# A two-layer kernel (cross-attention, then an RWKV block): the group norm's two head products as rounded passes, and a new order within a step

## The reference, cut to what matters

```python
xa = _ln(x, ln1_w, ln1_b)                       # layer norm over channels
sx = concat([state[:, 1:2] - xa[:, :1], xa[:, :-1] - xa[:, 1:]])
xxx = einsum(tanh((xa + sx * maa_x) @ maa_w1), maa_w2)
xk, xw, xv, xr, xg = xa + sx * (maa_stack + xxx)
w = exp(-exp(time_decay + tanh(xw @ td_w1) @ td_w2))
r, k, v = xr @ Wr.T, xk @ Wk.T, xv @ Wv.T;  g = silu(xg @ Wg.T)
out_t = r_t (u * k_t v_t + s);  s = k_t v_t + w_t * s      # scan over the tokens
m = og.mean(-1);  va = ((og - m) ** 2).mean(-1)            # og: out by heads of 16
og = (og - m) / sqrt(va + 1e-5) * gn_w + gn_b              # the group norm
x1 = x + (og * g) @ Wo.T
xc = _ln(x1, ln2_w, ln2_b); xk2, xr2 = mixes of xc and its shift
out = x1 + sigmoid(xr2 @ Wfr.T) * (square(relu(xk2 @ Wfk.T)) @ Wfv.T)
```

## Time and profile before

| what | value |
|---|---|
| median of three executions | 1414.32 us (1409.76 to 1417.7) |
| the profiled execution's own time | 1411.06 us |
| its span in the trace | 1409.2 us |
| granted TensorE clock, mean over the span | 0.981 of full speed |
| busy: TensorE / weight loads | 1329.8 us (94%) / 936.5 us (66%) |
| busy: VectorE, ScalarE, GpSimd | 929.5 us (66%), 734.7 us (52%), 492.5 us (35%) |
| chain that ended last, by engine | PE 80%, DVE 8%, issue 6%, DMA 3% |

### The profile page before, as it was taken

How to read it: one execution, slowest core, us unless ns; L and a number is a source line. 1 busy time by engine, 2 the same in 40 slices (tenths; PEclk the granted TensorE clock), 3 DMA queues, 4 the chain that set the end, 5 groups by cost and what they waited for, 6 DMA issues and landing times.

```text
span 1409.2 us, 42786 instructions
## 1 busy us (share of the span) xinstructions
PE 1329.8 (94%) x17120; PEld 936.5 (66%) x17120; DVE 929.5 (66%) x2431; ACT 734.7 (52%) x1772; POOL 492.5 (35%) x550
## 2 busy tenths in 40 slices
PE   4899999999999999987899999999999999999977
PEld 4677777777777777655666667666676667666634
DVE  3455555555555555456578878787888787887863
ACT  4676766766777666542334443545344534543332
POOL 2322222222222211113455345634554355534540
PEclk9999999999999999989899999999999999999979
DMA  5433322222222222213000010001000101010000
GB/s 169 138 94 106 100 69 69 71 75 75 75 75 75 75 69 65 89 43 135 21 21 10 26 28 21 13 24 27 21 14 22 27 22 27 9 27 21 15 14 13
DMA packets 47145, 73.70 MB, mean 52 GB/s; under 512 B 21413, under 2 KB 24101, under 8 KB 45445
## 3 DMA queue, kind: packets, MB, share of 16 engines
q1 hardware_dynamic: 46981, 71.24, 16.8%
HBM read 60.24 MB, written 7.57 MB: 48 GB/s over the span
## 4 chain that ended last, share of the span: by engine, by line
PE 80%; DVE 8%; issue 6%; DMA 3%; SPq 1%; ACT 1%; POOL 1%; DVEq 0%; ACTq 0%; POOLq 0%
PE b_bank L1824 18%; PE b_bank L1830 12%; PE ring_bank L696 6%; PE ring_bank L697 5%; PE ring_bank L698 5%; PE av_bank L782 4%; PE b_bank L1938 4%; PE score_banks L755 4%; DVE probs L443 3%; PE b_bank L1975 3%; PE score_banks L742 2%; PE b_bank L1964 2%; PE b_bank L1878 2%; DVE probsT L460 2%; PE av_bank L768 2%
## 5 line engine op out<-in xcount | busy, mean ns | idle before, releaser
L1119 POOL TENSOR_TENSOR rst<-rp,st 128x448 f32<-128x448 f32 x192 | 210.1, 1117 | 59.6 <-DVE st L1342 57.7
L443 DVE CUSTOM_DVE_ANT_0 probs<-score_banks,unmask 112x375 f32<-112x375 f32 x256 | 124.8, 545 | 93.0 <-issue 93.0
L588 ACT ACTIVATE probs<-probs,least_inv 112x375 f32<-112x375 f32 x256 | 152.4, 606 | 32.6 <-DVE least_inv L443 32.6
L460 DVE SCALAR_TENSOR_TENSOR probsT<-score_banks,least_cols 125x448 f32<-125x448 f32 x192 | 108.0, 618 | 54.4 <-PE score_banks L755 51.7
L603 ACT ACTIVATE probsT<-probsT,key_mask 125x448 f32<-125x448 f32 x192 | 114.6, 661 | 47.9 <-DVE probsT L460 47.7
L1111 POOL TENSOR_TENSOR xm<-mixed,xa 128x448 f32<-128x448 f32 x80 | 88.5, 1107 | 143.6 <-DVE mixed L1271 137.3
L337 POOL TENSOR_TENSOR aT_lo<-whole,aT_hi 128x375 fp32r<-128x375 f32 x64 | 58.9, 920 | 194.7 <-ACT whole L569 192.6
L696 PE MATMUL ring_bank<-aT_hi,wk_lo 128*128 128x376 f32 x256 | 91.2, 356 | 2.4 <-issue 2.4
L371 POOL TENSOR_TENSOR ctx_rstd<-ctx_var_eps,a_eps_exp 125x3 f32<-125x3 f32 x16 | 13.8, 864 | 214.6 <-DVE ctx_var_eps L416 214.6
L697 PE MATMUL ring_bank<-aT_lo,wk_hi 128*128 128x376 f32 x256 | 85.5, 334 | 0.0
L698 PE MATMUL ring_bank<-aT_hi,wk_hi 128*128 128x376 f32 x256 | 85.4, 334 | 0.0
(11 more groups left out here) (183 smaller groups left out, 3108.5 us busy)
## 6 DMA issues: line engine op xcount, KB each, us to landing
least_cols<-values_of_two_batches SPq DMA_DIRECT2D x32, 437.5 KB
ctx_tok<-in_ctx SPq DMA_DIRECT2D x16, 750.0 KB
xT_sb<-in_xT SPq DMA_DIRECT2D x16, 224.0 KB, 3.0
inv_cols<-values_of_two_batches SPq DMA_DIRECT2D x128, 28.0 KB, 4.1
x_tok<-in_x SPq DMA_DIRECT2D x16, 224.0 KB, 2.6
x_between_layers<-x_tok SPq DMA_DIRECT2D x16, 224.0 KB, 4.5
b_x<-x_between_layers SPq DMA_DIRECT2D x16, 224.0 KB, 3.0
x_post<-x_between_layers SPq DMA_DIRECT2D x16, 224.0 KB, 2.8
```

Source lines behind the costliest of these rows:

```text
L443: dve.tensor_tensor_reduce(out=probs[:, g % 2, i], in0=score_bank[0:T, i, 0:TC], in1=unmask[:, m[1]], scale=-SCALE, scalar=-LOWEST, op0=AL ...
L460: dve.scalar_tensor_tensor(out=probsT[:, g % 2, k].rearrange("p (i t) -> p i t", t=T), in0=score_bank[0:TK, :, k * T:(k + 1) * T], scalar= ...
L588: act.activation(probs[:, g % 2, i], probs[:, g % 2, i], ACT.Exp, scale=-1.0, bias=least_at(m, g, i), accum_out=sums[:, g, i:i + 1]).then_ ...
L1119: pool.tensor_tensor(by_chunk(rst[:, j % NPROD]), by_chunk(rp[:].rearrange("p c t -> p (c t)")), state_of(j), ALU.mult).then_inc(s_pprod, 1)
```

## The change

Both products of the group norm are made of two passes in the rounded float format (fp32r) instead of one float32 product. `wkv` is split: ScalarE's new `norm_high` rounds it, GpSimd's new `norm_low` subtracts the rounded part, and TensorE's `gn_centre` multiplies both parts with a matrix `centring` (identity minus head mean), which gives the centred values at once; `gn_mean` and VectorE's `centre` are gone. The squares are split in the same way: `square` and the new `square_high` on ScalarE, `square_low` on GpSimd, then two passes in `gn_var`. `x2` shares its memory with `x1_post` and `fin` with `ln2_tok`; two constants share a semaphore.

From step 3 on the lists within a step are also in another order, on all five engines. Steps 1 and 2 keep the old order (`early_step`), with the new calls put in.

```diff
+        centring = sb_first("centring", [P, P], F32R)
+        mean_r = sb_first("mean_r", [P, P], F32R)
...
         def step(n, pre, scan, post):
             m = later(n, -1)
-            if post:
-                l = later(n, -2)
-                if at_least(l, 1):
-                    sp.wait_ge(s_x2, count(later(l, -1), 1, 1))
-                sp.dma_start(x1p[:], A["x1"][index(l)]).then_inc(s_x1p[l[1]], 16)
             if pre and not is_batch(n, B - 1):
                 load_x1(later(n, 1))
             if post and at_least(n, 3):
                 store_out(later(n, -3))
+            l = later(n, -2)
+            if post and not is_last(l):
+                if at_least(l, 1):
+                    sp.wait_ge(s_fin, count(later(l, -1), 1, 1))
+                sp.dma_start(x1p[:], A["x1"][index(l)]).then_inc(s_x1p[l[1]], 16)
             if pre:
                 spread_value(n)
...
+        def norm_low(l):
+            pool.wait_ge(s_gnhi, count(l, 2, 1))
...
+            low, high = norm_parts(l)
+            pool.tensor_tensor(low, wkv[:], high.bitcast(F32), ALU.subtract).then_inc(s_gnlo, 1)
+
+        def square_low(l):
+            pool.wait_ge(s_sq, count(l, 1, 1))
+            pool.wait_ge(s_gnhi, count(l, 2, 2))
+            pool.tensor_tensor(norm_parts(l)[1], norm_home(l)[1], wkv_r[:].bitcast(F32), ALU.subtract).then_inc(s_gnlo, 1)
...
-        def centre(l):
-            dve.wait_ge(s_mean, count(l, 1, 1))
...
-            dve.tensor_tensor(norm_home(l)[0].rearrange("p c t -> p (c t)"), wkv[:].rearrange("p c t -> p (c t)"),
-                              norm_bank(l)[0][:, 0:CT], ALU.subtract).then_inc(s_cen, 1)
...
             if scans:
+                prefixes(m)
                 for d in range(2, CH + 1):
                     decay_key(m, d)
                 near_products(m, 0)
-                near_products(m, 1)
-                prefixes(m)
-                near_products(m, 2)
             if more:
                 stats1(p)
             if post:
                 wkv_sum(l)
             if scans:
+                near_products(m, 1)
                 decay_rec(m)
             if post and at_least(n, 3):
                 finish(later(n, -3))
...
+        def norm_high(l):
+            act.wait_ge(s_wkv, count(l, 1, 1))
...
+            act.copy(norm_parts(l)[1], wkv[:]).then_inc(s_gnhi, 1)
...
+        def square_high(l):
+            act.wait_ge(s_cen, count(l, 1, 1))
+            act.activation(wkv_r[:].rearrange("p c t -> p (c t)"), norm_bank(l)[0][:, 0:CT], ACT.Square).then_inc(s_gnhi, 1)
...
-                copy_vtok(n)
             if post:
                 xc_affine(l)
             if more:
                 xa_affine(p)
             if pre:
-                copy_rec(n)
                 tanh_gate(n)
+                copy_vtok(n)
             if post:
                 relu_square(l)
                 receptance(l)
...
-        def gn_mean(l):
-            pe.wait_ge(s_wkv, count(l, 1, 1))
+        def gn_centre(l):
...
+            pe.wait_ge(s_gnlo, count(l, 2, 1))
...
-            pe.matmul(norm_bank(l)[0][:, 0:CT], headmean[:], wkv[:].rearrange("p c t -> p (c t)"), start=True,
-                      stop=True).then_inc(s_mean, 1)
+            low, high = (x.rearrange("p c t -> p (c t)") for x in norm_parts(l))
+            pe.matmul(norm_bank(l)[0][:, 0:CT], centring[:], high, start=True, stop=False)
+            pe.matmul(norm_bank(l)[0][:, 0:CT], centring[:], low, start=False, stop=True).then_inc(s_cen, 1)
...
-            pe.matmul(norm_bank(l)[1][:, 0:CT], headmean[:], norm_home(l)[1].rearrange("p c t -> p (c t)"), start=True,
-                      stop=True).then_inc(s_var, 1)
+            pe.matmul(norm_bank(l)[1][:, 0:CT], mean_r[:], high, start=True, stop=False)
+            pe.matmul(norm_bank(l)[1][:, 0:CT], mean_r[:], low, start=False, stop=True).then_inc(s_var, 1)
```

More of the change, by code:

```diff
@@ L1149, in last_steps @@
             rec_key(m)
+            norm_low(l)
+            square_low(l)
             product(m, 0)
@@ L1180, in step @@
                 mix(n, 1)
-            if early:
                 rstd1(p)
+            if post:
+                norm_low(l)
+                square_low(l)
             if scan:
@@ L1211, in step @@
                 xa_state(p)
+        def step(n, pre, scan, post):
+            if is_batch(n, B):
+                return last_steps()
+            if is_batch(n, B + 1):
+                return
+            if is_batch(n, 1) or is_batch(n, 2):
+                return early_step(n, pre, scan, post)
+            p, m, l, more = later(n, 1), later(n, -1), later(n, -2), pre and not is_batch(n, B - 1)
+            if post:
+                norm_low(l)
+            if scan:
+                rec_key(m)
+            if pre:
+                mix(n, 0)
+            if post:
+                square_low(l)
+            if pre:
+                mix(n, 1)
+            if scan:
+                product(m, 0)
+                product(m, 1)
+            if more:
+                rstd1(p)
+            if scan:
+                product(m, 2)
+            if post:
+                gate_output(l, scan)
+            if pre:
+                mix(n, 2)
+                mix(n, 3)
+            if scan:
+                product(m, 4)
+                product(m, 5)
+                product(m, 6)
+                product(m, 8)
+            if post:
+                rstd2(l)
+            if pre:
+                mix(n, 4)
+            if scan:
+                product(m, 9)
+            if more:
+                xa_state(p)
+            if scan:
+                product(m, 10)
+                product(m, 12)
+                product(m, 13)
+                product(m, 14)
         def rest():
@@ L1779, in step @@
             if post:
+                square(l)
+                square_high(l)
                 gn_rstd(l)
@@ L2127, in step @@
                 ffn_value(l)
+        def step(n, pre, scans, post):
+            if is_batch(n, B):
+                return last_steps()
+            if is_batch(n, B + 1):
+                return
+            if is_batch(n, 1) or is_batch(n, 2):
+                return early_step(n, pre, scans, post)
+            p, m, l, more = later(n, 1), later(n, -1), later(n, -2), pre and not is_batch(n, B - 1)
+            if pre:
+                maa_second(n, (0, 1))
+            if scans:
+                transpose_keys(m)
+                bonus(m)
+            if post:
+                gn_centre(l)
+            if scans:
+                chunk_sums_free(m)
+                chunk_sums(m)
+            if pre:
+                decay_first(n)
+            if post:
+                gn_var(l)
+            if scans:
+                attend_near(m, 0)
+            if pre:
+                project(n, 1, "wv", s_vmm)
+            if scans:
+                attend_near(m, 1)
+                attend_near(m, 2)
+            if pre:
+                maa_second(n, (2, 3, 4))
+            if scans:
+                reduce(m, 0)
+                attend_near(m, 3)
+            if post:
+                project_out(l)
+            if pre:
+                decay_second(n)
+                project(n, 2, "wk", s_kmm)
+                project(n, 3, "wr", s_rmm)
+            if scans:
+                reduce(m, 1)
+            if more:
+                transpose_x(p)
+            if scans:
+                reduce(m, 2)
+            if post:
+                transpose_post(l)
+            if pre:
+                project(n, 4, "wg", s_gmm)
+            if scans:
+                reduce(m, 3)
+            if pre:
+                transpose_value(n)
+            if post:
+                ffn_key(l)
+                ffn_receptance(l)
+            if more:
+                maa_first(p)
+            if post:
+                ffn_value(l)
         def rest():
```

254 lines of the change are left out of this document (178 added, 76 removed).

## The result

The changed kernel took 1484.03 us (median of 4 executions, 1478.28 to 1485.47), the kernel before 1412.04 us beside it (1408.18 to 1417.7). The ratio is 1.0495 with a 95% interval of 1.0467 to 1.0524: 72 us or 5% slower. The forecast was 1470 us with 1440 to 1490.

What follows compares the result with a forecast made beforehand. TensorE's work was taken as the bound, 45.0 us a step, plus a late result's wait. 1411.06 + 62 (11 x 5.65) - 2.6 (gaining steps) + 2 (last step) = 1472.5, rounded down to 1470 us; range 1440 to 1490.

Steps and rivals of the forecast that it cites:

- The chain: From the value transposes through `vtok`, 13 transfers, the `b_x` load, `stats1`, `norm_low` and `rk` to `bonus`: 18.0 us.
- The wait: TensorE has 13.7 us of work against 18.0, so it waits 4.3 us ahead of `bonus`, for `rk`.
- GpSimd's two operations: `norm_low`'s subtraction and `rk`, in turn on GpSimd ahead of `bonus`, at 1.16 us each.
- The sentence in the prediction on the Trainium skill: VectorE and GpSimd block each other on SBUF; `norm_low` and `rec_key` may each be 0.25 us later, left out.
- the path of `mix(n, 0)` to `decay_first`: The mix reaches GpSimd about 7 us after the load, `decay_first` needs it some 8 us after: just covered.
- The clock: Behind TensorE's wait the granted clock falls to 0.5, costing 2.3 us a step (1.6 to 3.0).
- the likeliest case: Wait on TensorE and clock fall both come in each late step: 1458 to 1485 us; chance 0.60.
- the one in which it stays: TensorE's wait comes but the clock does not fall: 11 x 3.35 = 37, so 1447 us; chance 0.16.
- The period and the count: A step takes 51.6 us, 5.65 above before, in steps 4 to 14, 11 steps: +62 us.
- The last step's +2: In the last step `wkv`'s splits and a second `square_high` and `square_low` lie bare: +2 us (0 to +4).
- The products: A pair of rounded passes takes 0.60 us against 0.95 on TensorE; two pairs save 0.7 us a step.
- the first rival: The chain is under 13.7 us, TensorE stays full at 45.0 us a step: 1400 us, 0.8% faster; chance 0.10.

Runs made afterwards that it cites:

- experiment 10: Changed kernel with the x1 load a step ahead, fourth `attend_near` behind `project_out`, third and fourth `reduce` later: 1397.8 us, ratio 0.9902 to the kernel before.
- experiment 1: Changed kernel with SyncE loading x1 of batch n+2 in step n, ahead of the thirteen value transfers: 1408.92 us, ratio 0.9974 to the kernel before.
- 4: Changed kernel with `transpose_value` back between the `wk` and `wr` products and `copy_vtok` behind `copy_key`: 1410.65 us, ratio 0.9992 to the kernel before.
- experiment 2: Changed kernel with `rec_key` back ahead of `norm_low` in GpSimd's list: 1453.21 us, ratio 1.0269 to the kernel before.
- 5: Kernel before with only the value turned behind the last `reduce` and copied behind `tanh_gate`, from step 3 on: 1490.09 us, ratio 1.0543.
- experiment 6: Kernel before with the rounded two-pass group norm and its splits put into its old lists: 1433.71 us, ratio 1.0151.
- experiment 7: Kernel before with the rounded products in its old order, plus ScalarE's `spread_decay` moved ahead of `copy_keys`: 1412.53 us, ratio 0.9998.
- experiment 3: Changed kernel with five unused TensorE products between the key transposes and `bonus` in steps 3 to 14: 1460.48 us, ratio 1.0328 to the kernel before.

## Why the prediction was right

- **The bound.** TensorE's work set the step, and a late result could only add. Shown: with hardly a wait in its steps the new order is at 1398 us, with the long one it is at 1484. TensorE's work in a step was forecast as 45.0 us, and the mean period of experiment 10 is 45.1.
- **The chain.** It was forecast link by link, and stands so in the timeline after. From the value's transposes to the start of `stats1` 13.0 us were forecast, and 13.3 passed in the step shown (1043.42 to 1056.71), 12.8 in the mean of the eleven steps; from there to `bonus` 5.0 were forecast, and 5.4 and 5.5 passed. The sum was 18.0 and is 18.3 in the mean. Experiments 1 and 4 cut it at two places and each takes back all of the loss; 2 shortens it at its end; 5 makes it in the other kernel.
- **The wait.** 4.3 us forecast ahead of `bonus`, for `rk`; 4.6 in the mean of eleven steps.
- **What was undersized: GpSimd's two operations,** 1.16 each in the sum. `norm_low` took about 1.21 or 1.47, mostly in turns, and `rk` 1.60: 0.6 us more per step together; in experiment 1, with little beside them on VectorE, they took 1.14 and 1.17. In the changed kernel they run beside VectorE's near products, `decay_rec` and `finish`, some of which read two operands from SBUF. The sentence in the prediction on the Trainium skill ("SBUF — State Buffer", Who interferes with whom) had 0.5 of this, and I left it out of the sum. The trace agrees with the rule: also the mix took 2.76 us beside the scan in experiment 6, and 1.05 when experiment 7 moved it out of its way. It belongs in the sum. The load hid part of it by landing a little earlier than priced (2.6 us after its issue in the median, where 3.1 were taken).
- **What was left out: the wait for the near values,** 0.84 us a step at `attend_near` in the changed kernel. The prediction walked the path of `mix(n, 0)` to `decay_first` and found it just covered, which it was; it did not walk this one. The rest of a step, from `bonus` to the end of the next value's transposes, took 34.2 us where 33.6 were forecast with the clock.
- **The clock.** It fell in each of the eleven steps, as in the likeliest case, and not as in the one in which it stays. Priced at 2.3 us a step, it cost 2.2 by experiment 3 (52.47 against 50.26). The Trainium skill ("TensorE: Matmul & The Clock Gate", HAM oscillation) describes a kernel in which every tile waits for a DMA and the array is throttled again in each, and the trace agrees: `bonus` behind the wait took 1.76 us in ten of the eleven steps and 1.45 in one, where it takes 0.99 at full clock. That the price came out so near is partly luck: it was the middle of two unlike events, 1.6 and 3.0. And the prediction's sentence on waits of over 4 us has no row behind it: the only such wait in the trace before, 14.49 us at its start, was followed by a clock of 1.00. The length of one wait does not settle it either: waits of 1.60 to 2.87 us were followed by a fall in experiment 2, and one of 3.31 us at the end of the trace before (1394.61) was not.
- **The period and the count.** 51.6 forecast, 52.5 measured, over 11 steps: 10 of the 14 us between 1470 and 1484. Another 2.5 were the rounding down from 1472.5. The last step's +2 was +2.1.
- **The products.** 0.60 us a pair forecast, 0.61 measured. But the first rival, "the cover holds", assumed that without the chain the new order would reach 1400. It reaches 1409 (experiment 1): the new order had the wait of 0.9 us just named, and behind it one of 0.4 to 0.5.

What stays open: the old order with the products, which I expected to be the plain way to the gain, is not settled beyond experiment 7; its wait of 0.9 us for the sums was not removed. That VectorE's operations are what slowed GpSimd's is argued from what ran beside them; in experiments 1 and 7 they no longer met and GpSimd's were shorter, but other things had moved too, and no run took VectorE's operation alone away.

## What to carry to other kernels

- Before an operation is moved later in a pipelined step, follow everything that hangs behind it through the queues, the DMA queue above all, to the next step. A queue that is idle for 80% of a step can still be a link of the cycle: here 13 small transfers held up one load; experiment 1 issues it 11 us ahead of them (996.93 against 1007.88 in its trace). Follow the lists of the other engines too: `rk` did not need the load, it only stood behind an operation that did.
- A saving on the bounding engine of 1.5% of a step is smaller than any one wait of 1 us. Take the waits away one after the other and read the profile anew each time. Look also for small waits beside a long one: the one for the near values stood in the changed kernel's trace, and the one for GpSimd's products came up when it was gone.
- A recurring wait of 4 to 5 us on TensorE cost 2.2 us more in clock; count it in.
- Compare periods over many steps: short and long steps took turns here, and one pair gave 2.6 us for the clock where the mean of ten gives 2.2.

## What the runs showed of the hardware that was not expected

- Useless work on TensorE in a wait made the kernel 24 us faster (experiment 3), by holding the granted clock at 1.00.
- GpSimd's subtractions and products of 128 x 448 took between 1.05 and 2.76 us, and the long ones ran beside VectorE's work: 2.76 beside a scan of 2.06 us that started 0.14 us earlier. An engine at 50% load thus added 0.6 us to the chain of each step.
- In experiment 2 the granted clock fell in nine of eleven steps behind waits of 1.60 to 2.87 us.
